# One MoE block on one core: the end of the attention phase in an order of its own, and the first tile loads and pad writes on other engines

## The chip, the core and the metric

One program runs on one core of a Trainium2 chip. The core has a TensorE (matrix products, here PE), VectorE (DVE), ScalarE (ACT), GpSimd (POOL) and SyncE (SP, which here only issues transfers and waits). Each engine takes its own list of instructions in order; they are tied together by semaphores. SP, ACT and POOL issue DMA transfers. The metric is the device time of one execution in microseconds.

## The reference, cut to what matters

Input `x` has 16 images of 256 channels and 14 x 14 pixels. A convolution block runs first, then linear attention over the 196 pixels (tokens) of each image, then a mixture of experts (MoE) over all 3136 tokens. The kernel computes every token for its two chosen experts only.

```python
x = _L0_conv_ref(x, ...)                       # conv 1x1, 3x3, 1x1 with batch norms, residual
t = _to_tokens(x)                              # (16, 196, 256)
t = t + _L1_attn_ref(_ln_t(t), w_qkv, w_out, b_out)   # linear attention, 16 heads of 16
t = t + _L1_ffn_ref(_ln_t(t), gate_w, gate_b, w1, b1, w2, b2)
x = _from_tokens(t, x)

def _L1_ffn_ref(x, gate_w, gate_b, w1, b1, w2, b2):   # E = 8 experts, 1024 hidden columns
    probs = softmax(flat @ gate_w + gate_b)
    top_p, top_i = top_k(probs, 2)
    top_w = top_p / (sum(top_p) + 1e-9)
    for e in range(8):
        h = gelu(flat @ w1[e] + b1[e])
        out = out + comb[:, e:e + 1] * (h @ w2[e] + b2[e])
```

## The kernel before, in words

**Phase A** goes over the 16 images in a software pipeline. Slot `n` of the loop does stage `in` of image `n`, `norm` of `n - 1`, `qkv` of `n - 2`, `soft` of `n - 3`, `ctx` of `n - 4`, `out` of `n - 5`, `norm2` of `n - 6` (the table `LAG`). So in slots 16 to 24 images run out: fewer and fewer stages are left, and the loop keeps its distances. The stages of one image form a chain: `ctx` on PE (L759, 4 matmuls), masked on DVE (`cT`, L1103), `proj` on PE (L768), copied by ACT (`pr`, L578), `out` on PE (L775), added by DVE (`img`, L1110), statistics on DVE (L1027), an inverse root by 13 short dependent DVE steps (L1047 to L1066), normalised by ACT into `rows` (L535), turned on PE (L787), copied by ACT (`xT`, L583), gate logits on PE (L797).

Images go in pairs to the **routing** of a group g = 0 to 7 (392 tokens): `route_choose` on DVE (L1141 to L1148), an exponential on ACT (L587), `route_top` on DVE (L1156 to L1195: the two experts, the count per expert `run`), `route_rank` on PE (L805 to L810), `route_slots` on DVE (L1202 to L1215). A slot is the row of the DRAM table `rows_by_expert` to which a token's row goes. `send_rows` on POOL (L442) then scatters the group by 8 indirect DMAs of 98 rows of 265 floats. Group g is scattered under semaphore number g mod 4.

**The tile table.** When all counts are known, DVE works out in a chain of small instructions (`tile_table`, L1226 to L1296) where each expert's rows end (`pad_at`), at which column of the table each of the 56 tiles of 128 rows lies (`tbi[:,1]`), how many of the first four tiles are full without the last group (`late`, `latei`), each tile's expert (`tbi[:,0]`), and the packed list for PE and DVE (`packedi`, `is_expert`). Behind each expert's last row, 128 rows of `padrow` are written so that the last tile of an expert has defined rows: SP does this with 8 plain DMAs (L353, L354), each behind a register load of its address.

**Phase B** takes the 56 tiles, sorted by expert. For tile m: ACT loads its rows (`load_rows`, L616 to L627, three tiles ahead), PE turns them (`x_turn`, L837), ACT rounds them (`xrTh`, L633), DVE forms the rest (`xrTl`, L1360), PE multiplies by the first matrix (`hidden`, L844, in three parts), DVE adds the bias (L1375), ACT applies gelu (L638), PE turns the result (L871), ACT and DVE split it, PE multiplies by the second matrix (`expert_out`, L844), DVE finishes, POOL adds the rows into the output (L464). PE slot m does `h_turn(m-2)`, `x_turn(m)`, `hidden(m-1)`, `expert_out(m-2)`.

On ACT the loads of tiles 0, 1 and 2 stand ahead of the first `turned` (L633). Each of them reads three values into registers (one from `tbi`, two from `latei`) and waits on semaphores by those values: a tile that is not full without the last group waits for that group's scatter and for all the pads, a full one for neither. By the reference's own routing the first expert gets 936 of the 6272 rows (8 tiles), 718 of them from groups 0 to 5. So tiles 0 to 4 are full without groups 6 and 7, and tile 7 is the expert's last, with 40 rows.

PE starts phase B only when the whole table is done (`s_tab` at `TAB_STEPS`).

## Time and profile before

| | us |
|---|---|
| median of 3 runs without profile | 713.14 (710.79 to 713.86) |
| the profiled execution's own time | 718.35 |
| its span, first to last instruction | 716.6 |
| TensorE, granted clock over the span | 0.923 |

Outside the span lie 1.75 us. The profiled execution took 5.21 us more than the median. Times of the trace count from the start of the span. A row of the time line gives start, duration, engine, line, operation, output<-input, how many such instructions are merged, and in brackets how long the engine was idle before it and who ended that.

### The profile page before, as it was taken

To read this page: it belongs to the slowest core of one execution; us is meant where nothing else is said; L and a number is where in the kernel's file an instruction comes from. 1 tells how busy PE (TensorE), PEld (TensorE's weight loads), DVE (VectorE), ACT (ScalarE), POOL (GpSimd) and SP (SyncE) were. 2 spreads that over 40 slices of the span, in tenths; PEclk is the share of its full clock that TensorE was granted. 3 is DMA by queue.
4 is the path that set the end of the run, shared out by engine and by line. 5 is a ranking of instruction groups with operands and counts; after the bars stand their busy time and mean duration, and the time that the engine had idled before them with its cause. 6 is when DMAs were issued, how large, how long until landed. Compare 5 with 4: busy or idle time off the path is not lost.

```text
span 716.6 us, 13723 instructions
## 1 busy us (share of the span) xinstructions
PE 618.5 (86%) x3884; PEld 544.8 (76%) x3884; DVE 455.6 (64%) x1484; ACT 320.1 (45%) x624; POOL 218.3 (30%) x194
## 2 busy tenths in 40 slices
PE   7664699999999965239999999999999999999982
PEld 3642578888788854228999999999999999999972
DVE  2867879999997864515565565565565565565550
ACT  1475678878775522104343334334334334334330
POOL 6040233224655564621221212221131221221220
PEclk9887699999999985559999999999999999999996
DMA  9418878988979841231246383744726628322211
GB/s 252 155 59 293 335 295 308 316 305 296 329 261 369 336 147 52 87 104 31 46 145 203 49 299 47 248 100 95 253 45 169 187 39 289 67 39 46 31 16 15
DMA packets 50197, 121.09 MB, mean 169 GB/s; under 512 B 7308, under 2 KB 38864, under 8 KB 43984
## 3 DMA queue, kind: packets, MB, share of 16 engines
q1 hardware_dynamic: 30368, 98.54, 38.1%
q0 software_dynamic: 11136, 14.00, 11.5%
q10 hardware_dynamic: 8624, 7.68, 4.1%
q8 instruction: 38, 0.62, 0.3%
q14 instruction: 31, 0.25, 0.1%
HBM read 68.09 MB, written 52.11 MB: 168 GB/s over the span
## 4 chain that ended last, share of the span: by engine, by line
PE 65%; DVE 16%; issue 6%; DMA 4%; ACT 3%; SPq 2%; DVEq 0%; another core or an unknown queue 0%; POOL 0%; ACTq 0%; POOLq 0%
PE ps L844 44%; PE ps L871 6%; DMA wset<-in_ew 3%; DVE wset L1116 3%; PE ps L683 2%; PE ps L738 2%; PE ps L693 2%; PE ps L837 2%; DVE stt L1027 1%; DMA img<-in_x 1%; PE ps L768 1%; PE ps L759 1%; PE ps L775 1%; DVE cT L1103 1%; SPq L353 1%
## 5 line engine op out<-in xcount | busy, mean ns | idle before, releaser
L464 POOL DMA_INDIRECT out<-ys,xr x56 | 86.7, 1548 | 309.2 <-DVE ys L1386 235.8
L844 PE MATMUL ps<-wset,hTh 128*128 x896 | 163.0, 283 | 3.5 <-DVE hTl L1354 3.4
L844 PEld LDWEIGHTS ps<-wset,hTh 128*128 128x128 f32 x896 | 141.6, 190 | 10.2 <-issue 5.5
L844 PE MATMUL ps<-wset,xrTh 128*128 x448 | 146.6, 408 | 0.0
L638 ACT ACTIVATE hb<-hb 128x512 f32<-128x512 f32 x112 | 70.4, 633 | 133.5 <-DVE hb L1375 133.2
L844 PE MATMUL ps<-wset,hTl 128*128 x448 | 126.3, 282 | 0.0
L644 ACT CAST hTh<-ps 128x512 fp32r<-128x512 f32 x112 | 60.3, 590 | 99.1 <-PE ps L871 98.6
L1381 DVE TENSOR_TENSOR yb<-ps,bset 128x256 f32<-128x256 f32 x56 | 23.8, 425 | 125.1 <-PE ps L844 125.1
L844 PEld LDWEIGHTS ps<-wset,xrTh 128*128 128x128 f32 x448 | 80.8, 190 | 15.7
L844 PE MATMUL ps<-wset,xrTl 128*128 x224 | 89.1, 398 | 0.0
L1375 DVE TENSOR_TENSOR hb<-ps,bset 128x512 f32<-128x512 f32 x112 | 75.5, 686 | 16.6 <-PE ps L844 16.3
L844 PEld LDWEIGHTS ps<-wset,hTl 128*128 128x128 f32 x448 | 85.0, 190 | 0.0
L1354 DVE TENSOR_TENSOR hTl<-ps,hTh 128x512 fp32r<-128x512 f32 x112 | 71.8, 683 | 11.5 <-ACT hTh L644 8.7
L442 POOL DMA_INDIRECT rows_by_expert<-rows,slot x64 | 62.4, 975 | 31.1 <-issue 16.6
L418 POOL TENSOR_TENSOR img<-img,bo 98x512 f32<-98x512 f32 x16 | 29.1, 1816 | 109.5 <-ACT xh L535 105.9
L738 PE MATMUL ps<-xT,wq 128*128 128x196 f32 x256 | 51.5, 346 | 12.6 <-ACT vT L557 9.9
L871 PE MATMUL ps<-ident,hb 128*128 128x128 f32 x448 | 58.3, 273 | 0.9 <-ACT hb L638 0.9
L738 PEld LDWEIGHTS ps<-xT,wq 128*128 128x128 f32 x256 | 45.1, 198 | 18.1 <-ACT xT L552 9.6
L871 PEld LDWEIGHTS ps<-ident,hb 128*128 128x128 f32 x448 | 50.2, 141 | 1.6 <-ACT hb L638 1.6
L844 PEld LDWEIGHTS ps<-wset,xrTl 128*128 128x128 f32 x224 | 42.5, 190 | 10.3
L837 PE MATMUL ps<-ident,xr 128*128 128x128 f32 x112 | 22.0, 279 | 20.9 <-DVE packedi L1293 12.5
L775 PE MATMUL ps<-pr,vT 128*98 128x256 f32 x128 | 32.7, 401 | 1.5 <-ACT pr L578 1.5
(196 smaller groups left out, 948.3 us busy)
## 6 DMA issues: line engine op xcount, KB each, us to landing
split_weights<-wset SPq DMA_DIRECT2D x16, 2048.0 KB
wset<-split_weights SPq DMA_DIRECT2D x32, 1024.0 KB
wset<-in_ew SPq DMA_DIRECT2D x16, 1024.0 KB, 10.6
xr<-rows_by_expert ACTq DMA_DIRECT2D x56, 132.5 KB, 2.2
bset<-in_eb SPq DMA_DIRECT2D x8, 640.0 KB
out<-img SPq DMA_DIRECT2D x16, 196.0 KB
img<-in_x SPq DMA_DIRECT2D x6, 392.0 KB, 7.2
rows_by_expert<-padrow SPq DMA_DIRECT2D x9, 132.5 KB
```

Of the source, the lines that this page charges most:

```text
L418: pool.tensor_tensor(t, t, bo2[:, :, :].rearrange("p j d -> p (j d)"), ALU.add).then_inc(S["norm"]["pool"], 1)
L442: pool.indirect_dma_start(norm_rows, bass.IndirectOffsetOnAxis(slot[:, g % 2, k, t:t + 1], 0), rows[:, at, h, :], None).then_inc(s_rows[g ...
L464: pool.indirect_dma_start(out, bass.IndirectOffsetOnAxis(xr[:, r % XR, C + E:ROW].bitcast(U32), 0), ys[:, r % YS, :], None, compute_op=ALU ...
L638: act.activation(hb[:, p, h * 512:(h + 1) * 512], hb[:, p, h * 512:(h + 1) * 512], ACT.Gelu).then_inc(s_ge, 1)
L644: act.copy(hTh[:, p, h * 512:(h + 1) * 512], ps[:, 3 + h, :]).then_inc(s_hhi, 1)
L738: last = pe.matmul(dst[:, h * HW:(h + 1) * HW], wq[:, k, off + h * 128:off + (h + 1) * 128], xT[:, p, k, :], start=(k == 0), stop=(k == 1))
L775: last = pe.matmul(psC[0:HALF, j * C:(j + 1) * C], vT[:, i % 3, h, j * HALF:(j + 1) * HALF], pr[:, i % 2, h, :], start=(h == 0), stop=(h = ...
L837: last = pe.transpose(ps[:, 0, k * 128:(k + 1) * 128], xr[:, b, k * 128:(k + 1) * 128], ident[:, :])
L844: last = pe.matmul(dst, rows_k[:, k * 128:(k + 1) * 128], wset[:, bass.ds(column(k) + rest, width)], start=(k == 0 and n == 0), stop=(k == ...
L871: last = pe.transpose(ps[:, 3 + h, k * 128:(k + 1) * 128], hb[:, p, h * 512 + k * 128:h * 512 + (k + 1) * 128], ident[:, :])
L1354: V.tensor_tensor(hTl[:, p, part], ps[:, 3 + h, :], hTh[:, p, part].bitcast(F32), ALU.subtract).then_inc(s_hlo, 1)
L1375: V.tensor_tensor(hb[:, p, h * 512:(h + 1) * 512], ps[:, 1 + h, :], bset[:, bass.ds(off + h * 512, 512)], ALU.add).then_inc(s_hb, 1)
```

## The change

What it does:

1. **The end of phase A.** The slot loops of PE, ACT and DVE stop at `n = 17` (`TAIL`). What slots 18 to 24 did for images 12 to 15 is written out per engine. `ctx` of image 15 uses its own PSUM bank and stands right behind `proj` of image 14; `proj` of 14, `out` of 15 and `xT` of 15 use other banks too; images 14 and 15 are normalised together. `ones2` and `both` of the routing get two buffers each, and the steps `pos` to `slots` a semaphore of their own.
2. **The flags of the first four tiles** now count rows without the last two groups. Column and flag of two tiles are packed into one integer (`sooni`). ACT loads the two integers, then per tile only waits by the flag and raises `s_soon`; SP issues the loads of tiles 0 to 3, each when its flag is up, and then those of 4 to 7, all of which wait for groups 6 and 7 and for all pads. ACT issues loads from tile 8 on.
3. **The pads** go to POOL: 8 indirect DMAs of 128 rows, in its order behind the last scatter. The pad row block that SP wrote at the start is written by POOL too.
4. **The table.** PE and DVE start phase B when columns and experts are there (`TAB_EXPERTS`, 25 steps). What follows (`schedule_table`) DVE does behind the first tile's `xrTl`; PE waits for `TAB_STEPS` ahead of its fifth slot.

```diff
             sp.wait_ge(s_const, NCONST)
-            sp.dma_start(norm_rows[128 * NONE:128 * (NONE + 1), :], padrow[:, :]).then_inc(s_ends, 16)
...
-            sp.wait_ge(s_ends, 16)
-            sp.wait_ge(s_tab, 1)
-            for e in range(E):
-                at = sp.value_load(pad_at[0:1, e:e + 1], min_val=0, max_val=128 * (NONE - 1))
-                sp.dma_start(norm_rows[bass.ds(at, 128), :], padrow[:, :]).then_inc(s_ends, 16)
-            sp.wait_ge(s_tab, TAB_STEPS)
+            sp.wait_ge(s_tab, TAB_ROWS)
+            soon_two = [sp.value_load(sooni[0:1, n:n + 1], ...) for n in range(SOON // 2)]
+            for i in range(SOON):
+                one = soon_two[i // 2] >> (8 * (i % 2))
+                sp.wait_ge(s_soon, i + 1)
+                load_rows(sp, one & 127, i)
+            for a in range(2, RING // 2):
+                sp.wait_ge(s_rows[a], 256)
+            sp.wait_ge(s_ends, 16 + 16 * E)
+            for i in range(SOON, XR):
+                load_rows(sp, sp.value_load(tbi[0:1, 1, i:i + 1], ...), i)
+            sp.wait_ge(s_tab, TAB_EXPERTS)
...
             send_rows(B // 2 - 1, 1)                                  # gpsimd
+            pool.wait_ge(s_tab, TAB_PADS)
+            for e in range(E):
+                pool.indirect_dma_start(norm_rows, bass.IndirectOffsetOnAxis(pad_at[:, e:e + 1], 0),
+                                        padrow[:, :], None).then_inc(s_ends, 16)
...
-            for i in range(3):                                        # scalar
-                load_rows(i, i)
+            for a in range(2):
+                act.wait_ge(s_rows[a], 256)
+            act.wait_ge(s_tab, TAB_ROWS)
+            soon_two = [act.value_load(sooni[0:1, n:n + 1], ...) for n in range(SOON // 2)]
+            for i in range(SOON):
+                more = (soon_two[i // 2] >> (8 * (i % 2))) & 128
+                for a in range(2, RING // 2):
+                    act.wait_ge(s_rows[a], more + 128)
+                act.wait_ge(s_ends, more + 16)
+                act.sem_inc(s_soon, 1)
...
+            G = B // 2 - 1                                            # tensor
+            out_out(LAST - 2)
+            route_rank(G - 3)
+            norm2_logits(LAST - 4)
+            soft_kT(LAST)
+            ctx_ctx(LAST - 1)
+            ctx_proj(LAST - 1)
+            ctx_ctx(LAST)
+            norm2_xT(LAST - 3)
+            out_out(LAST - 1)
+            ctx_proj(LAST)
+            norm2_logits(LAST - 3)
+            out_out(LAST)
+            route_rank(G - 2)
+            pe.matmul(psV[:, E:2 * E], ones[:, :], run[:, (G - 1) % 2, :], start=True, stop=True)
+            norm2_xT(LAST - 2)
+            norm2_logits(LAST - 2)
+            norm2_xT(LAST - 1)
+            norm2_xT(LAST)
+            norm2_logits(LAST - 1)
+            norm2_logits(LAST)
+            route_rank(G - 1)
+            pe.matmul(psV[:, 0:E], ones[:, :], run[:, (G + 1) % 2, :], ...).then_inc(s_cntp, 1)
+            route_rank(G)
...
-            pe.wait_ge(s_tab, TAB_STEPS)
+            pe.wait_ge(s_tab, TAB_EXPERTS)
...
+            out_add(LAST - 1)                                         # vector
+            wait_for(dve, "out", "vec", "add", LAST - 1)
+            stats("norm2", 1, LAST - 1, n + 2)
+            out_add(LAST)
+            wait_for(dve, "out", "vec", "add", LAST)
+            stats("norm2", 0, LAST, n + 2)
+            beside(inverse_roots(n + 2, 0, 2), route_slots(G - 2))
+            drain(chains[1])
+            drain(route_choose(G - 1))
+            drain(route_top(G - 1))
+            drain(route_choose(G))
+            beside(route_top(G), route_slots(G - 1))
+            drain(chains[1])
+            beside(route_slots(G), tile_table())
+            drain(chains[1])
+            dve.wait_ge(s_tab, TAB_EXPERTS)
...
+                if m == 0:
+                    drain(schedule_table())
```

How it stands on the engines: a name with `<-` is output and input, `x3` is how many like it follow, and the waits are the semaphores of other engines. PE before, from `out` of image 14:

```order
L775 MATMUL ps<-pr,vT 98x256 [waits ctx_steps_of_act]
L775 MATMUL ps<-pr,vT 98x256 x3
L797 MATMUL ps<-gw,xT 98x8 [waits route_steps_of_vec,norm2_steps_of_act]
L797 MATMUL ps<-gw,xT 98x8 x3
L759 MATMUL ps<-qn,ekt 128x128 [waits out_steps_of_vec,soft_steps_of_pool,soft_steps_of_act]
L759 MATMUL ps<-qn,ekt 128x128 x3
L768 MATMUL ps<-wo,cT 128x256 [waits soft_steps_of_act,ctx_steps_of_vec]
L768 MATMUL ps<-wo,cT 128x256
L787 MATMUL ps<-ident,rows 128x98 [waits norm2_steps_of_act]
L787 MATMUL ps<-ident,rows 128x98 x3
L775 MATMUL ps<-pr,vT 98x256 [waits ctx_steps_of_act]
L775 MATMUL ps<-pr,vT 98x256 x3
```

PE now, from `proj` of image 14:

```order
L813 MATMUL ps<-wo,cT 128x256 [waits in_steps_of_act,ctx_steps_of_vec]
L813 MATMUL ps<-wo,cT 128x256
L799 MATMUL ps<-qn,ekt 128x128 [waits soft_steps_of_vec,soft_steps_of_pool,soft_steps_of_act]
L799 MATMUL ps<-qn,ekt 128x128 x3
L841 MATMUL ps<-ident,rows 128x98 [waits route_steps_of_vec,gate_steps_of_act,norm2_steps_of_act]
L841 MATMUL ps<-ident,rows 128x98 x3
L824 MATMUL ps<-pr,vT 98x256 [waits ctx_steps_of_act]
L824 MATMUL ps<-pr,vT 98x256 x3
L813 MATMUL ps<-wo,cT 128x256 [waits soft_steps_of_act,ctx_steps_of_vec]
L813 MATMUL ps<-wo,cT 128x256
L851 MATMUL ps<-gw,xT 98x8 [waits route_steps_of_vec,gate_steps_of_act]
L851 MATMUL ps<-gw,xT 98x8 x3
```

`ctx` of image 15 (the row with `qn,ekt`) has moved ahead of `out` of image 14 and has lost its wait for DVE's add of image 14.

ACT before, behind its last instruction of phase A (`latei` holds the flags):

```order
L616 TENSOR_LOAD tbi [waits rows_sent_to_experts2,rows_sent_to_experts1,padding_written,rows_sent_to_experts0,table_steps]
L616 ISA x2
L618 TENSOR_LOAD latei
L618 ISA x2
L618 TENSOR_LOAD latei
L618 ISA x2
L627 ISA [waits expert_ends_padded,rows_sent_to_experts3]
L627 DMA xr<-rows_by_expert 128x265
```

ACT now at the same place (one tile's flag; three more follow, then `xrTh` of tile 0):

```order
L688 TENSOR_LOAD sooni [waits table_steps,rows_sent_to_experts1,rows_sent_to_experts0]
L688 ISA x2
L688 TENSOR_LOAD sooni
L688 ISA x2
L692 REGISTER_ALU x2
L693 REGISTER_ALU [waits rows_sent_to_experts3,rows_sent_to_experts2]
L692 REGISTER_ALU [waits expert_ends_padded]
```

The three address and flag loads per tile and the DMA issue are gone from ACT; two loads for all four tiles are left.

POOL now, from the last group's scatter:

```order
L464 DMA rows_by_expert<-rows,slot 26752x265 [waits place_steps_of_vec,token_numbers_written]
L464 DMA rows_by_expert<-rows,slot 26752x265 x7
L478 DMA rows_by_expert<-padrow,pad_at 26752x265 [waits table_steps]
L478 DMA rows_by_expert<-padrow,pad_at 26752x265 x7
L489 DMA out<-ys,xr 3264x256 [waits residual_written,padding_written,expert_rows_ready]
```

Between the scatter and the first add of expert rows now stand the eight pad writes.

## Rows read from the trace of the kernel before

**Rows 1.** The page: the span, and the granted clock in 40 slices of it:

```profile
span 716.6 us, 13723 instructions
...
PEclk9887699999999985559999999999999999999996
```

**Rows 2.** The chain that ended last (start, us): turning of tiles 1, 4, 5:

```profile
317.18 0.66 PE ps L837 x2
...
338.63 0.22 PE ps L837 x2
...
345.39 0.22 PE ps L837 x2
```

**Rows 3.** The time line, tiles 0 to 2: loads, turning, first rounding:

```profile
304.51 11.58 ACTq L627 DMA_DIRECT2D xr<-rows_by_expert  x3
...
308.16 0.69 PE L837 MATMUL ps<-ident,xr 128*128 128x128 f32 x2 [12.54 <-DVE packedi L1293]
...
316.13 0.37 ACT L633 CAST xrTh<-ps 128x256 fp32r<-128x256 f32 x1 [24.36 <-DMA rows_by_expert<-padrow]
```

**Rows 4.** The instructions on xr from 294 to 345: landing of tile loads:

```profile
DMA to landing us min/median/max: 2.0/2.6/3.9
```

**Rows 5.** Instructions by line, min/median/max ns: register work and pad writes from 294 on:

```profile
L618 ACTq TENSOR_LOAD <-latei x2: 278/280/282, 303.2 to 303.7; - x2
...
L618 ACTq TENSOR_LOAD <-latei x1: 1396/1396/1396, 308.1 to 308.1; - x1
...
L354 SPq DMA_DIRECT2D rows_by_expert<-padrow x8: 3/332/700, 298.1 to 316.3; - x8
```

**Rows 6.** The time line, PE, DVE and ACT at the end of phase A:

```profile
254.36 0.61 DVE L1103 SCALAR_TENSOR_TENSOR cT<-ps,kx,heads 128x128 f32<-128x128 f32 x2 [0.84 <-PE ps L759]
...
255.02 1.87 PE L768 MATMUL ps<-wo,cT 128*128 128x256 f32 x4 [1.55 <-DVE cT L1103]
...
260.94 1.13 PE L759 MATMUL ps<-qn,ekt 98*128 98x128 f32 x8 [0.26 <-DVE img L1110]
...
264.97 0.61 DVE L1103 SCALAR_TENSOR_TENSOR cT<-ps,kx,heads 128x128 f32<-128x128 f32 x2 [1.56 <-remote]
...
269.83 3.73 PE L775 MATMUL ps<-pr,vT 128*98 128x256 f32 x8 [1.47 <-ACT pr L578]
...
280.09 0.35 DVE L1047 TENSOR_SCALAR sm<-mv 98x2 f32<-98x2 f32 x1
...
280.09 1.50 PE L797 MATMUL ps<-gw,xT 128*98 128x8 f32 x8 [0.57 <-ACT xT L583]
...
283.38 0.16 DVE L1066 SCALAR_TENSOR_TENSOR sm<-mv,sm 98x2 f32<-98x2 f32 x1 [0.17 <-DVE sm L1063]
284.15 1.09 ACT L535 ACTIVATE rows<-img,sm 98x256 f32<-98x256 f32 x2 [4.11 <-DVE sm L1066]
...
292.67 0.17 DVE L1191 TENSOR_TENSOR run<-run,rv 98x8 f32<-98x8 f32 x1
...
295.65 0.19 DVE L1202 TENSOR_TENSOR rt<-ps,expert_row 98x32 f32<-98x32 f32 x1 [2.69 <-issue]
```

**Rows 7.** The time line, DVE in the tile table:

```profile
300.32 0.16 DVE L1267 TENSOR_SCALAR latei<-late 128x4 int32<-128x4 f32 x1
300.51 0.69 DVE L1271 TENSOR_REDUCE tb<-big 128x64 f32<-128x512 f32 x1
```

**Rows 8.** The time line, POOL: scatters, first of groups 5 and 7, last:

```profile
276.97 0.97 POOL L442 DMA_INDIRECT rows_by_expert<-rows,slot  x1 [9.29 <-DVE slot L1215]
...
300.67 0.98 POOL L442 DMA_INDIRECT rows_by_expert<-rows,slot  x1 [0.30 <-POOL rows L435]
...
309.53 0.96 POOL L442 DMA_INDIRECT rows_by_expert<-rows,slot  x1 [0.30 <-issue]
```

**Rows 9.** The page: all scatters (L442) and adds (L464), mean ns in the middle:

```profile
L464 POOL DMA_INDIRECT out<-ys,xr x56 | 86.7, 1548 | 309.2 <-DVE ys L1386 235.8
...
L442 POOL DMA_INDIRECT rows_by_expert<-rows,slot x64 | 62.4, 975 | 31.1 <-issue 16.6
```

More of the change, by code:

```diff
@@ L546, in norm2_norm @@
                     act.wait_ge(s_rows[g % (RING // 2)], 128 * (g // (RING // 2) + 1))
-                normalise("norm2", 1, i, n, [rows[:, i % RING, j, 0:C] for j in range(2)])
+                normalise("norm2", which, i, n, [rows[:, i % RING, j, 0:C] for j in range(2)])
             def norm_xT(i):
@@ L780, in norm2_xT @@
                 wait_for(pe, "norm2", "act", "norm1", i)
-                wait_for(pe, "norm2", "act", "xT", i - 1)
+                bank = psL
+                if i < LAST:
+                    wait_for(pe, "gate", "act", "xT", i - 1)
+                else:
+                    bank = psT
+                    wait_for(pe, "ctx", "act", "proj", LAST - 1)
                 if i % 2 == 0:
@@ L1121, in over, with step @@
                 return v.unsqueeze(2).to_broadcast([HALF, 4, k])
[L1123 to L1127 removed]
+            L, comb, pos = rt[:, 0], rt[:, 5], rt[:, 6]
+            def step(name, g, reads=None, stage="route"):
                 if reads is not None:
[L1129 to L1134 removed]
+                    wait_for(dve, stage, "vec", reads, g)
+                done_r[stage] += 1
+                assert after(stage, "vec", name, g) == done_r[stage]
+                return S[stage]["vec"], 1
+            done_r = {"route": 0, "place": 0}
             def route_choose(g):
                 v = rv[:, g % 2]
[L1139 removed]
+                wait_for(dve, "gate", "pe", "logits", 2 * g + 1)
                 sig = step("bias", g)
@@ L1204, in route_slots @@
                 yield
-                sig = step("prods", g, "pos")
+                sig = step("prods", g, "pos", "place")
                 V.tensor_tensor(rt[:, 7:9], pos.unsqueeze(1).to_broadcast([HALF, 2, 4, E]), ones2,
@@ L1299, in tile_table @@
                 dve.wait_ge(s_tab, tab[0])
-            for n in range(SLOTS_A):
+            for n in range(TAIL):
                 i = {stage: n - LAG[stage] for stage in LAG}
```

223 lines of the change are left out of this document (140 added, 83 removed).

## The prediction

> **What bounds the kernel now.** I read the page first. The span is 716.6 us, and the granted clock stands at five tenths from slice 15 to 17, that is from about 268 to 322 us: full clock 2.4 GHz, there 1.2 [rows 1]. That stretch is the end of phase A and the start of phase B, the place of the change. Behind it everything runs in a fixed beat: the chain that ended last turns tile 4 at 338.63 and tile 5 at 345.39, one tile in 6.76 us [rows 2], to the end. No instruction of that beat is changed. So the whole question is when the beat starts, and the marker is the turning of tile 1, at 317.18 [rows 2].
>
> What holds tile 1 back? Tile 0 was turned at 308.16 already, yet ACT rounded it only at 316.13 [rows 3], because ACT was still issuing loads: three of them spread from 304.51 to 316.09 [rows 3]. One register load of ACT takes 278 ns at 303 us and 1396 ns at 308 [rows 5]; SP's eight pad writes stretch from 298.1 to 316.3 [rows 5]; the two-matmul turn of tile 0 shows 0.69 us where those of tiles 4 and 5 show 0.22 [rows 2, 3]. I call this the **crawl**: from about 300 to 313 us several engines advance in steps of 0.7 us. It goes on just as long as POOL scatters group 7, from 300.67 to 310.49 [rows 8], and a little longer. Ahead of it, the table of tiles waits for the counts: `run` of group 7 is written at 292.67, its `pos` at 295.65 [rows 6], the flags at 300.32 [rows 7]. ACT gets free of its waits at about 302, when group 6 has landed.
>
> **The change part by part.** The sum is made in times of the profiled execution (718.35, 1.75 outside the span); that one is 5.21 above the median of 713.14.
>
> *Order of the tail.* `proj` of image 14 ends at 255.02 + 1.87 = 256.9 [rows 6]. `ctx` of image 15 stood at 260.94, behind the add of image 14 [rows 6]; now it follows `proj` directly. Its 1.13 us may double to 2.1 at the lower clock, and DVE sees it 0.84 later, so `cT` of image 15 comes at 260.0 and not 264.97 [rows 6]: 5.0 earlier. From there: `proj` 15 (1.9, copy 0.9, waits 1) and `out` 15 (3.73 [rows 6]) put the add at about 269, both statistics at 270.7. The 13 root steps take 283.54 - 280.09 = 3.4 [rows 6]: 274.1. Two images are normalised one behind the other, 2 x 1.09 [rows 6]: 276.4. Turning, copying and the logits of 14 and 15 (1.50 each [rows 6], halves overlapping): 280.3. The rank product of group 6 stands ahead on PE, 1.9: 282.2. Top-two work of group 7 to `run`: 285.7, against 292.84, so 7 us gained; `pos`, 2.8 behind it as before (2.98 - 0.17 [rows 6]): 288.5.
>
> *The table.* From `pos` to the flags 300.48 - 295.65 = 4.8 before [rows 6, 7]. One reduction of 0.69 [rows 7] now stands ahead of the flags, and a packing step of about 0.2: 5.75, hence 294.2.
>
> *First load.* ACT waits only for groups 4 and 5 for tiles 0 to 3 (the reference's counts fill those tiles without the last two groups), reads two integers of 0.28 each [rows 5] with their register work (1.4 in all, estimated from three reads and an issue per tile at the uncrawled rate), checks the flag (0.5); SP issues (0.3) and the rows land 2.6 later, the middle of 2.0 to 3.9 [rows 4]: tile 0 is turned at 299.0. ACT has no loads left in front of its rounding. Before, rounding to the next turn took 317.18 - 316.13 = 1.05 [rows 2, 3], the turn itself and its lag 0.5 more: **tile 1 is turned at 300.4 and not 317.18, 16.8 earlier.** Of this 7 is the tail, less 1 for the longer table; the other 10.7 is ACT's wait for group 6 and the crawl over its nine reads and three issues.
>
> *What is moved behind tile 0 on DVE* (`schedule_table`, some 15 small instructions, 2.6) lies under the first hidden product, whose operands DVE has given up by then; PE asks for it only ahead of its fifth slot. Nothing. If the cover fails it costs at most 2.6.
>
> *POOL.* The scatter of group 5 waited 9.29 for its slots at 276.97 [rows 8]; with slots at 271.6 it starts at 272.1. A group takes 309.53 + 0.96 - 300.67 = 9.82, 0.3 between instructions [rows 8], plus the copies: group 5 to 282.2, group 6 283.9 to 294.0, group 7 294.5 to 304.6. Then eight pads of 128 rows. None is in this trace. By the mean scatter of 98 rows, 975 ns [rows 9], unscaled: 0.98 + 0.3 = 1.28 each, the floor. By the mean add of 128 rows, 1548 ns [rows 9]: 1.85, the ceiling. I take the scatter scaled by rows, 975 x 128/98 + 300 = 1.57, as the same kind of write: 8 x 1.57 = 12.6, to 317.2 (314.8 to 319.4). They land 2.0 later as a load's minimum does [rows 4], SP reads and issues 0.6, tile 4 lands 2.6 later: 322.4. Its turn falls due at 338.63 - 16.8 = 321.8. So the gate of tile 4 costs 0.6 (below zero at the floor, 2.8 at the ceiling, up to 4.7 if landing also takes its longest). POOL's adds start behind the pads at 317.2; the first result comes two tiles after 300.4, near 316, so they are late by a microsecond or two, and ring buffers absorb that.
>
> Here a rule speaks against the change. SP issued the first two pads, before the crawl, about 2 us apart, and one write shows 332 ns of issue in the middle [rows 5]; POOL's nearest kind shows 975 [rows 9]. The Trainium skill (DMA: Bandwidth & Descriptors, "Issuing engine by pattern") puts plain stores on Sync and says of the two ways that the one from SP and ACT is "generally faster". By that rule the pads left on SP would finish with group 7's landing, tile 4 would have 11 us to spare, and the 0.6 of the gate would be 0; the sum hardly moves, the risk does.
>
> Sum in the profiled execution: -16.8 + 0.6 = **-16.2**, 702.1.
>
> *From the profiled execution to the median.* The profiled one is 5.21 slower, by more than the 3.07 that the three runs span. Outside the crawl nothing in the trace looks stretched, so I take those 5.2 us to be the crawl, absent or weaker in the timed runs. The changed kernel has its first four loads issued by 297 and would not pay it; the timed gain is then 16.2 - 5.2 = 11.0, and the median **702.1**. In words of the skill: the Trainium skill (NOTIFIC — the notification-queue block, "7.1 Overflow: three behaviours, one of which stalls the engine") says that the record path's inner pipeline always backpressures and can throttle an engine; that would make the crawl the profiler's own. No row here proves it.
>
> **The rivals.** *(a) The crawl is real* and is in the timed runs too; the 5.2 is some other overhead of a profiled run. Then the median falls by the full 16.2, or 15 to 19 with the landing bounds: 694 to 698, say 697. For it: the crawl coincides with scatters, and earlier groups' scatters may do the same unseen. Against: the earlier scatters from 276.97 to 300.1 run beside ACT and DVE rows of ordinary length (0.16, 0.17, 1.09 [rows 6]).
>
> *(b) The crawl is real and lies on POOL's write stream behind the table, wherever that is.* It begins about when the table is read and ends with POOL's last scatter. POOL's stream now ends not at 310.5 but with the eighth pad, at 317.2, and the crawl ends 2.5 to 3.7 behind it (before, it held ACT until 316.1 with scatters ending at 310.5). If it holds ACT's two reads, four flag checks and the rounding in the same way, tile 1 is turned at 319 to 321 and not 317.2: 3.7 us **slower**, 716.8. It decides from the point where the crawl reaches back before 297. Against: ACT has 2 reads to make, not 9, and SP only 2; even at 1.4 us each they cost 2 more.
>
> *(c) POOL is the bound:* pads at or above the ceiling of 1.85, or groups 5 to 7 late because the tail gains less than 5 on DVE's side. Then tile 4 comes at 327 to 330 and the beat starts late by 5 to 8: 706 to 710. For it: my margin is below zero already. It holds too where SP's waits, in program order, hold the loads of tiles 4 to 7 all together, so that the last of them comes 2 us later still.
>
> *(d) The tail doesn't move:* DVE, which now does both adds, both statistics and the top-two work of group 5 in one written order, or PE at half clock, is late, and `run` stays at 292.8. Then tile 1 still comes at 307.5, POOL stays as it was and its pads end at 323: tile 4 at 328.5, late by 0 against 338.63 - 10 = 328.6; gain 10 in the profile, 5 in the median: 708.
>
> **How the numbers follow.** The forecast of 702.1 (its own range 699 to 706: the landing 2.0 to 3.9, the pads 1.28 to 1.85, the tail +-2) gets 0.46. (a) 0.22, (c) 0.14, (d) 0.09, (b) 0.09. The range reaches from 695 (inside (a)) to 710 (inside (c)); outside it are (b) and the edges of (a) and (c), together 0.2. A measurement of this kernel can tell about 0.5%, 3.6 us, from no change, so faster means below 709.6: the forecast, (a), (d) and nearly all of (c), 0.84 with a rest for what I have not seen; within 0.5%: part of (c), of (d) and half of (b), 0.09; slower 0.07.
>
> **What would show it.** In the profile of the changed kernel: `cT` of image 15 near 260 (order of the tail); `run` of group 7 near 285.7; SP's first load near 296.5; tile 1 turned near 300.4; ACT's register loads at 0.28, or at 1.4 if the crawl has come along; eight pad writes on POOL from 304.6 to 317.2, their mean the number that I bounded; a wait of PE or ACT at tile 4 of a microsecond or none; the first adds near 317. If tile 1 is turned early and tile 4 late, it is (c); if tile 1 is at 307, (d); if it is at 319, (b). The excess of the profiled execution over the median says whether the crawl was the profile's: near 0 for my reading, near 5 for (a). I am wrong altogether if the beat of 6.76 itself changes, or if the low clock lasts longer into phase B.

## The result and the profile after

The changed kernel took 715.36 us (713.32 to 717.67, 20 runs), the kernel before 711.69 in 20 runs beside it. The ratio, formed over the rounds, is 1.0042, interval 1.0028 to 1.0056: 3.0 us slower (the two medians lie 3.7 apart). The forecast was 702.1 and faster; the time lies outside the range of 695 to 710. What came is the size of rival (b): slower by 3.7.

The page of the kernel after, its span and the granted clock:

```profile
span 714.7 us, 13676 instructions
...
PEclk9987799999989986568999999999999999999997
```

The clock is granted at or near its lower level (1.2 GHz, five and six tenths) in about the same place as in [rows 1]. The time line of the kernel after, all engines, from 299 to 325 us (`issue` and `remote` in the brackets mean that the view names no engine or transfer of this core that ended the wait):

```profile
299.79 26.09 SPq L268 DMA_DIRECT2D xr<-rows_by_expert  x8
...
302.18 0.66 PE L917 MATMUL ps<-ident,xr 128*128 128x128 f32 x2 [11.05 <-DMA xr<-rows_by_expert]
...
306.20 0.37 ACT L660 CAST xrTh<-ps 128x256 fp32r<-128x256 f32 x1 [18.62 <-DMA rows_by_expert<-rows,slot]
...
307.25 0.66 PE L917 MATMUL ps<-ident,xr 128*128 128x128 f32 x2 [4.41 <-DVE xrTl L1493]
...
308.84 1.49 POOL L478 DMA_INDIRECT rows_by_expert<-padrow,pad_at  x1 [0.30 <-issue]
...
311.31 0.40 PE L924 MATMUL ps<-wset,xrTl 128*128 x1
...
311.47 0.68 DVE L1508 TENSOR_TENSOR hb<-ps,bset 128x512 f32<-128x512 f32 x1
...
318.29 0.96 POOL L478 DMA_INDIRECT rows_by_expert<-padrow,pad_at  x1 [0.30 <-issue]
321.69 0.69 DVE L1508 TENSOR_TENSOR hb<-ps,bset 128x512 f32<-128x512 f32 x1 [9.54 <-remote]
...
324.01 0.63 PE L917 MATMUL ps<-ident,xr 128*128 128x128 f32 x2
```

Read it from the top. Tile 0 is turned at 302.18, 6.0 earlier than in [rows 3], tile 1 at 307.25, 9.9 earlier than in [rows 2]. Then all is lost again. PE's last product of tile 0's hidden layer ends at 311.7. DVE adds the bias to the first half at 311.47 and is free at 312.15. The second half waits by the program for that product alone, and DVE takes it up only at 321.69, 9.5 us late. ACT and PE still work off the first half, until 313.5; from then on to 321.5 nothing runs but POOL and SP's last steps. POOL's eighth pad is issued at 318.29 and ends at 319.25; 2.4 us later the work goes on. Tile 2 is turned at 324.01, 16.8 behind tile 1; before, it followed by 6.7, at 323.8. The chain of the kernel after shows where the beat begins:

```profile
324.22 0.43 PE ps L917 x2
...
340.15 0.22 PE ps L917 x2
```

The last row is tile 4: 340.15 against 338.63 [rows 2], 1.5 later. From there the beat is 6.72 a tile, as it was before from tile 5 on.

The same thing on a smaller scale stands at the end of phase A. The time line of the kernel after, DVE and PE around the logits of the last two images:

```profile
277.71 2.72 PE L851 MATMUL ps<-gw,xT 128*98 128x8 f32 x16
...
285.17 0.19 DVE L1224 TENSOR_TENSOR rt<-ps,gb 98x32 f32<-98x32 f32 x1 [5.34 <-remote]
...
288.59 0.18 DVE L1275 TENSOR_TENSOR run<-run,rv 98x8 f32<-98x8 f32 x1
```

The logits end at 280.4, and DVE takes them up at 285.17, 4.7 later. POOL's scatters of group 5 run from 273.98 to 283.7. I call this, and the crawl of the prediction, the **hold**.

The lines of SP's loads in the kernel after, one form each (min/median/max ns, first and last start):

```profile
L268 SPq DMA_DIRECT2D xr<-rows_by_expert x7: 6/333/700, 299.8 to 324.5; - x7
L268 SPq ALU_OP  x6: 3/358/1397, 299.0 to 310.3; - x6
```

The steps of 0.7 and 1.4 us of [rows 5] are there again, now on SP. They go on to 315. Yet the hold is not there at every moment of POOL's run. POOL writes without a break from 298.80 to 319.25, and between 306.2 and 313.5 ACT, DVE and PE hand work to each other at their usual pace; DVE's eight small steps of the schedule (307.02 to 308.7) come 0.2 apart. In the kernel before, DVE's steps at that place stood 0.7 apart. What starts and ends a single held stretch is not shown.

### The profile page after: what moved, and what is told of

The parts are those of the page before. It is cut to its first block, busy times and chain, and to the rows that moved or that the text cites. A ratio compares the mean times of both kernels' runs of the same rounds, so it can differ in the third digit from the quotient of the medians.

```text
span 714.7 us, 13676 instructions
## 1 busy us (share of the span) xinstructions
PE 616.1 (86%) x3884; PEld 544.1 (76%) x3884; DVE 456.0 (64%) x1471; ACT 320.1 (45%) x624; POOL 228.7 (32%) x205
## 4 chain that ended last, share of the span: by engine, by line
PE 67%; DVE 19%; issue 5%; ACT 2%; another core or an unknown queue 2%; DMA 2%; DVEq 1%; POOL 0%; SPq 0%; ACTq 0%; POOLq 0%
PE ps L924 43%; PE ps L951 7%; DVE wset L1199 3%; PE ps L773 2%; PE ps L718 2%; PE ps L728 2%; PE ps L708 2%; DVE stt L1108 2%; PE ps L917 2%; PE ps L799 2%; DMA wset<-in_ew 1%; PE ps L824 1%; PE ps L762 1%; DVE cT L1185 1%
## 5 line engine op out<-in xcount | busy, mean ns | idle before, releaser
L464 POOL DMA_INDIRECT rows_by_expert<-rows,slot x64 | 61.5, 961 | 30.3 <-issue 16.9
L951 PE MATMUL ps<-ident,hb 128*128 128x128 f32 x448 | 58.7, 274 | 10.7 <-ACT hb L665 10.7
L440 POOL TENSOR_TENSOR img<-img,bo 98x512 f32<-98x512 f32 x16 | 30.7, 1919 | 110.5 <-ACT xh L560 110.5
L773 PE MATMUL ps<-xT,wq 128*128 128x196 f32 x256 | 51.6, 347 | 12.2 <-ACT vT L582 10.9
L773 PEld LDWEIGHTS ps<-xT,wq 128*128 128x128 f32 x256 | 45.1, 199 | 17.7 <-ACT xT L577 9.4
L924 PEld LDWEIGHTS ps<-wset,xrTl 128*128 128x128 f32 x224 | 42.8, 191 | 10.4
L762 PE MATMUL ps<-wq,xT 128*98 128x256 f32 x128 | 33.9, 412 | 0.0
```

Source lines behind the costliest of these rows:

```text
L440: pool.tensor_tensor(t, t, bo2[:, :, :].rearrange("p j d -> p (j d)"), ALU.add).then_inc(S["norm"]["pool"], 1)
L464: pool.indirect_dma_start(norm_rows, bass.IndirectOffsetOnAxis(slot[:, g % 2, k, t:t + 1], 0), rows[:, at, h, :], None).then_inc(s_rows[g ...
L762: last = pe.matmul(psQ[0:HALF, j * C:(j + 1) * C], xT[:, p, k, j * HALF:(j + 1) * HALF], wq[:, k, 0:C], start=(k == 0), stop=(k == 1))
L773: last = pe.matmul(dst[:, h * HW:(h + 1) * HW], wq[:, k, off + h * 128:off + (h + 1) * 128], xT[:, p, k, :], start=(k == 0), stop=(k == 1))
L924: last = pe.matmul(dst, rows_k[:, k * 128:(k + 1) * 128], wset[:, bass.ds(column(k) + rest, width)], start=(k == 0 and n == 0), stop=(k == ...
L951: last = pe.transpose(ps[:, 3 + h, k * 128:(k + 1) * 128], hb[:, p, h * 512 + k * 128:h * 512 + (k + 1) * 128], ident[:, :])
```

## The experiments

All ratios are against the kernel before, timed on the same chip in the same rounds. The other columns, in us, are from one profiled execution each: the start of group 5's first write, and the turning of tiles. That execution and the timed median can differ by a few microseconds; the ratio decides.

The column of group 5 shows why. Six of these kernels have the same program up to that write, but for buffers set aside and a constant written at the start: before, before with 8 more, with 8 more of 16 rows, with 8 more paced, with pauses by four, and with POOL busy otherwise. Still it comes anywhere from 270.4 to 277.0, and the profiled execution of the kernel before is the latest. The profiled executions of the six lie above or below their own medians nearly in that order: 270.4 (-3.4 us), 271.9 (-1.6), 272.2 (-2.4), 272.9 (-0.9), 275.3 (+3.0), 277.0 (+5.2, or +6.7 by all 20 runs). So when two kernels are compared by their tiles, what they already differ by in this column comes off first. (The gaps of work put 1.8 us of POOL's own work ahead of it.)

| kernel | ratio (95% interval) | group 5 | tile 1 | tile 2 | tile 4 |
|---|---|---|---|---|---|
| before | 1 | 277.0 | 317.2 | 323.8 | 338.5 |
| after | 1.0042 (1.0028 to 1.0056) | 274.0 | 307.2 | 324.0 | 340.0 |
| after, pads on SP | 0.9887 (0.9858 to 0.9916) | 273.5 | 307.9 | 315.7 | 330.3 |
| after, 8 more writes | 1.0159 (1.0129 to 1.0189) | 273.3 | 309.0 | 326.0 | 349.3 |
| before, new tail alone | 0.9988 (0.9969 to 1.0007) | 271.1 | 312.3 | 320.0 | 334.7 |
| before, 8 more writes | 1.0104 (1.0074 to 1.0134) | 271.9 | 321.5 | 328.3 | 343.1 |
| before, 8 more of 16 rows | 1.0117 (1.0080 to 1.0155) | 272.9 | 322.4 | 330.3 | 345.0 |
| before, 8 more, paced | 1.0021 (0.9995 to 1.0048) | 272.2 | 315.0 | 322.8 | 337.5 |
| pads on SP, group 7 later | 0.9854 (0.9819 to 0.9888) | 274.2 | 304.3 | 312.0 | 326.8 |
| pads on SP, old tail | 0.9957 (0.9930 to 0.9984) | 272.6 | 310.0 | 317.2 | 331.8 |
| **pads on SP, pauses by four** | **0.9788 (0.9755 to 0.9821)** | 271.2 | 296.3 | 303.4 | 318.0 |
| before, pauses by four | 0.9967 (0.9944 to 0.9991) | 270.4 | 306.8 | 314.4 | 329.0 |
| after, pauses by four | 0.9975 (0.9953 to 0.9997) | 271.9 | 297.0 | 303.9 | 331.8 |
| before, POOL busy otherwise | 0.9996 (0.9972 to 1.0020) | 275.3 | 314.8 | 321.6 | 336.2 |
| pads on SP, pauses by eight | 0.9859 (0.9822 to 0.9896) | 273.7 | 303.7 | 311.2 | 326.1 |
| pads on SP, gaps of work | 0.9816 (0.9786 to 0.9846) | 275.1 | 299.6 | 306.5 | 324.8 |

### Where the time went: pads, stream or tail

**The pads back on SP.** The edit is which engine writes them (the block written at the start too):

```diff
                 load_rows(sp, one & 127, i)
+            for e in range(E):
+                at = sp.value_load(pad_at[0:1, e:e + 1], ...)
+                sp.dma_start(norm_rows[bass.ds(at, 128), :], padrow[:, :]).then_inc(s_ends, 16)
...
-            for e in range(E):                                        # gpsimd
-                pool.indirect_dma_start(norm_rows, ... pad_at[:, e:e + 1] ..., padrow[:, :], None).then_inc(s_ends, 16)
```

> The changed kernel, but the eight pads are plain DMAs of SP again, issued behind its loads of tiles 0 to 3 (the first pad block at the start is SP's too). Theory A (the crawl): SP, DVE and ACT are held as long as POOL's stream of indirect writes runs; it now ends with group 7 near 308.5, so the crawl ends near 311 and not at 321.5, tile 2 is turned near 314 to 316 and not at 324.0, tile 4 near 332: 7 to 8 us faster than the changed kernel, about 708, 3 to 4 faster than before. Theory B (only the gate of tiles 4 to 7 decides, the crawl is the profile's own): the pads on SP land near 317 to 318 and not 321, tile 4 comes 3 earlier at most: about 712 to 713. Theory C (the tail's new order alone makes the kernel slow): still 715.

Measured 0.9887: by the ratios 8.1 us faster than before and 11 faster than the changed kernel. This is theory A's number and more; the gate alone (theory B) would have given 3. The chain of this kernel:

```profile
307.87 0.66 PE ps L916 x2
...
315.83 0.22 PE ps L916 x2
...
330.42 0.22 PE ps L916 x2
```

Tile 1 is turned at nearly the same time as in the changed kernel (0.6 later), tile 2 8.3 earlier. POOL's stream ends at 308.4 here. The eight pads stand on SP from 311.4 to 320.2, behind the hold, at 1.1 us each.

**Eight more writes**, which nobody reads or waits for, in the kernel after and in the kernel before:

```diff
+            for e in range(E):
+                pool.indirect_dma_start(spare[e], ... padrow[0:128, C + E:ROW] ..., padrow[0:128, :], None).then_inc(s_extra, 16)
```

> The changed kernel with eight further indirect writes of 128 rows on POOL, into tables that nobody reads, behind the pads; only POOL itself waits for them, at its own end. Theory A: the crawl lasts 10.2 us longer, to about 331.7; tile 2 is turned near 334; about 10 us slower than the changed kernel, 725. Theory B: nobody waits for them, and POOL's first add is not due before 333: 715, no change.

> The kernel before with eight further indirect writes of 128 rows on POOL behind the last scatter, into tables that nobody reads; only POOL waits for them, at its own end. Theory A: the crawl ends at about 323 and not 313, tile 1 is turned near 327 and not 317; about 10 us slower than before, 721.5. Theory B: nobody waits for them and POOL's first add is due only near 330: 711.7, no change.

Measured 1.0159 and 1.0104. Against the changed kernel the first is 1.17% or 8.3 us slower, the second 7.4 us slower than before. Theory B said no change. The expected 10 us were a little too many, and the expected place was wrong: in the kernel after, tile 2 came through at 326.0 and not at 334, and the further hold fell on tile 3 (341.4). Its time line:

```profile
323.67 0.69 DVE L1514 TENSOR_TENSOR hb<-ps,bset 128x512 f32<-128x512 f32 x1 [9.70 <-remote]
...
333.50 1.07 ACT L677 CAST hTh<-ps 128x512 fp32r<-128x512 f32 x2 [8.47 <-remote]
```

POOL writes without a break here until 328.7. DVE was let go in the middle of that run, work went on to 330.9, and ACT took up PE's next result only 4.8 us behind the run's end. So a longer run makes more hold, but one held stretch need not end with the run. In the time line of the kernel before with eight more, ACT issues its three loads here:

```profile
300.01 20.41 ACTq L633 DMA_DIRECT2D xr<-rows_by_expert  x3
```

20.4 us for three loads, where [rows 3] has 11.6. Nothing was changed on ACT. POOL's last of the eight starts at 314.40. Tile 1 is turned 4.3 later than before, though group 5 had begun 5.1 earlier.

**The tail alone**: the kernel before with the new order of PE, ACT and DVE and, but for what the flags count, nothing else of the change (the diff is the part of the change above from `G = B // 2 - 1` to `tile_table()`).

> The kernel before with the new order of the end of phase A alone: loads of tiles by ACT, pads by SP and the whole table ahead of phase B as before (the flags count without the last two groups, which changes none for tiles 0 to 3). Theory A: the counts of group 7 come 4 us earlier (288.8 against 292.8), group 7's scatters end near 308.5 and not 310.5, the crawl near 311 and not 313: tile 1 turned near 315, 2 us faster than before, about 709.7. Theory B: tile 1 is earlier by the 4 us of the counts: 707.7. Theory C: slower than before by 3.

Measured 0.9988, an interval that holds 1. In the profiled execution tile 1 came 4.8 earlier and tile 4 3.7, but group 5 had begun 5.9 earlier already; the timed runs show 0.9 us, not told from zero. Theory C (the tail makes it slow) is out. **The pads on SP with the old tail** is the other half of that question (the diff is e1's without the order of the tail; ACT there waits for the flags, as in the change):

> The version with the pads on SP, but with the old order of the end of phase A: loads by SP, flags without the last two groups, the rest of the table behind tile 0. The counts come 3 to 4 us later again, and so do group 7's scatters (end 310.5). If the gain of the pads-on-SP version is that ACT has no addresses and loads to work through in the hold, it keeps most of it: 0.992 of before (5 to 6 us faster). If the tail's order is what brings it, it is 0.997 or worse.

Measured 0.9957, between the two expectations. So loads by SP with the short flags are worth 3 us without the new tail (interval 1 to 5), and the tail 5 us more (0.9957 to 0.9887) once the loads no longer stand in its way. Together they give 8 us, more than the 4 of each alone; by the intervals the difference is between 1 and 7.

### What in POOL's stream does it

**Short writes, paced writes, no writes**, all in the kernel before, all behind the last scatter:

```diff
-    ... padrow[0:128, C + E:ROW] ..., padrow[0:128, :], None)         # eight more
+    ... padrow[0:16, C + E:ROW] ..., padrow[0:16, :], None)           # of 16 rows
```

```diff
+                if e:                                                 # paced
+                    pool.wait_ge(s_extra, 16 * e)
```

```diff
+            for e in range(16):                                       # busy otherwise
+                pool.tensor_scalar(idle[:, 1, :], idle[:, 0, :], 2.0, None, ALU.mult).then_inc(s_extra, 1)
+                pool.wait_ge(s_extra, e + 2)
```

> As the run with eight further writes of 128 rows in the kernel before (which took 1.04% more than it), but each of the eight writes only 16 rows, an eighth of the bytes and descriptors. If the hold comes from POOL being at work on indirect writes at all, and one of 16 rows takes POOL about as long as one of 98 or 128 (0.96 and 0.97), it still costs 7 to 8 us: 719. If it comes from the bytes or the number of rows, about 1 us: 712.5. If a short write is issued in half the time, 3 to 4 us and the hold still ends with the stream.

> The kernel before with eight further writes of 128 rows as before, but each waits until the one ahead has landed (some 3.3 us apart, to about 335). If any write of POOL under way holds the others, the hold lasts until about 337 and the time grows by more than with the unpaced ones, over 10 us. If only a stream without gaps holds them, no more than 0 to 3 us are lost.

> The kernel before with POOL busy for about 10 us behind the last scatter, with sixteen small products of its own on 128x512 elements and no writes. If it is indirect writes that hold the others, no change: 1.000 of before. If any work of POOL does, about 7 us slower, 1.010.

Measured 1.0117, 1.0021 and 0.9996. A write of 16 rows takes POOL 0.85 and not 0.97, and costs the others the same, so it is neither the bytes nor the rows. The same eight writes at a distance of 3 us cost nothing that can be told from zero. And POOL at its own work costs nothing, though its sixteen products, each waiting for the one ahead, took 25.1 us and not 10:

```profile
308.96 25.14 POOL L458 TENSOR_SCALAR idle<-idle 128x512 f32<-128x512 f32 x16
```

SP's steps show the same in the profiles. Its own pad writes from 312 us on, in the kernels with eight more writes, with paced ones and with POOL busy otherwise, in this order:

```profile
L356 SPq MOVE rows_by_expert<-padrow x4: 3/29/688, 312.0 to 321.1; - x4
...
L356 SPq MOVE rows_by_expert<-padrow x2: 29/29/29, 312.2 to 313.3; - x2
...
L356 SPq MOVE rows_by_expert<-padrow x3: 29/29/29, 312.1 to 314.2; - x3
```

Only in the first do steps of 0.7 us go on behind 312 (the last on any engine starts at 318.4); in the other two the last starts at 310.3, 4.8 and 1.4 us behind the end of the last scatter, though POOL's paced writes go on to 329 and its products to 334.

What holds the others is an **unbroken run of indirect writes on POOL**.

### Breaking the stream

**Group 7 later** sends the last group only once tile 1 is turned; **pauses by four** wait for the landing of the four writes ahead:

```diff
+                if g == B // 2 - 1 and j == 0:                        # group 7 later
+                    pool.wait_ge(s_eT, 2)
```

```diff
+                if g >= B // 2 - 3:                                   # pauses by four
+                    if j:
+                        pool.wait_ge(s_rows[g % R], 128 * (g // R) + 64)
+                    else:
+                        pool.wait_ge(s_rows[(g - 1) % R], 128 * ((g - 1) // R + 1))
```

> The version with the pads on SP (0.989 of before), but POOL sends group 7 only once tile 1 is turned. Theory A1 (writes hold engines that wait, and hardly those that work): nothing is held between 298 and the turning of tile 1, which comes near 303 and not 307.9; group 7 goes out beside the running beat, to 313, tile 4 loads near 318, due 325: 5 us faster than the version with the pads on SP, about 0.982 of before. Theory A2 (writes hold everybody at any time): tile 1 comes near 303, but tile 2 is held until about 315: about the same as the pads on SP, 0.989.

> The version with the pads on SP, and POOL's stream broken in groups 5 to 7: ahead of each four writes it waits until those before have landed, 2 to 3 us each time. If only an unbroken stream holds the others, the hold near 282 (3.6 us, PE to DVE) and that near 300 to 307 both go: the counts come 3 us earlier, tile 1 is turned near 300; group 7 ends near 317 and tile 4 loads near 323, where it may wait 2 us. 6 us faster than the pads on SP alone: 0.980 of before. If the pauses only delay the groups, tile 4 is late by 8 and it is no faster than before.

Measured 0.9854 and 0.9788. The second is 15 us faster than the kernel before and 18 faster than the changed one. In group 7 later, tile 1 comes at 304.3, and the eight writes run beside the beat from 305.84 to 316.14 with little harm (tile 2 at 312.0, and tile 3 at 319.7, 7.7 behind it, where the version with pauses has 6.8; theory A1). With the pauses both holds are gone. The time line of the version with pauses:

```profile
277.70 0.19 DVE L1229 TENSOR_TENSOR rt<-ps,gb 98x32 f32<-98x32 f32 x1 [0.70 <-PE ps L856]
...
281.80 0.17 DVE L1280 TENSOR_TENSOR run<-run,rv 98x8 f32<-98x8 f32 x1
...
292.20 2.34 SPq L268 DMA_DIRECT2D xr<-rows_by_expert  x4
294.59 0.66 PE L922 MATMUL ps<-ident,xr 128*128 128x128 f32 x2 [10.26 <-DMA xr<-rows_by_expert]
...
296.33 0.66 PE L922 MATMUL ps<-ident,xr 128*128 128x128 f32 x2 [1.08 <-issue]
```

DVE takes up the logits 0.7 after it is free, and not 5.3. `run` of group 7 is written at 281.80: 10.9 earlier than in [rows 6], 6.8 earlier than in the changed kernel; of these, 5.8 and 2.8 were there at group 5's first write, ahead of the first pause that cost anything. SP issues four loads in 2.34 us. Tile 1 follows tile 0 by 1.7. This is the kernel without the hold that the prediction's sum describes, except that here the pads are on SP.

The same pauses in the two given kernels:

> The kernel before with these pauses alone. If only an unbroken stream holds the others: ACT works through its loads at 1.1 us each from about 305 (group 6 lands later by 3), tile 1 is turned near 309 to 311 and not 317; tile 4 waits for group 7, which lands near 320: 4 to 6 us faster than before, 0.993. If not: slower by the pauses' 3 to 6 us.

> The changed kernel with the pauses in groups 5 to 7 and in the pads too. The hold goes, tile 1 comes near 300 and tile 2 near 308 and not 324; but the pads now end near 333, tiles 4 to 7 load near 337, so tile 4 is turned near 339 by the gate alone, as in the changed kernel (340.0): within 2 us of it. That would say that pads on POOL cannot win either way.

Measured 0.9967 and 0.9975. The hold is gone from both profiles (tile 1 at 306.8 and 297.0). In the kernel before the timed gain is 2.3 us, less than expected, though the profiled execution had tile 4 9.4 earlier. The column of group 5 settles that difference: 6.6 us of it were there ahead of the first pause that cost anything, and 2.8 remain. In the changed kernel, where the pauses also stand ahead of the first and the fifth pad, the pads on POOL become the gate, plainly. Its chain:

```profile
325.87 2.60 DMA rows_by_expert<-padrow,pad_at
...
329.28 2.52 DMA xr<-rows_by_expert
...
331.85 0.69 PE ps L925 x2
...
341.59 0.22 PE ps L925 x2
```

Tile 3 was turned at 310.7. Tile 4 waits 21 us for the last pad, its landing and its own load, and PE, idle for 13 us, is back near the lower clock (0.69 granted on average from 331 to 342, 1.00 from 342 to 350), so that tile 5 takes 9.7. So with the hold the pads on POOL cost 11 us of the timed ratio, by the hold, and without it 13, by the gate.

**How long a run it takes, and what ends it:**

```diff
-                if g >= B // 2 - 3:
-                    if j: ... else: ...
+                if g >= B // 2 - 3 and j == 0:                        # pauses by eight
+                    pool.wait_ge(s_rows[(g - 1) % R], 128 * ((g - 1) // R + 1))
```

```diff
+                if g >= B // 2 - 3:                                   # gaps of work, ahead of each four
+                    pool.tensor_scalar(idle[:, 1, :], idle[:, 0, :], 2.0, None, ALU.mult).then_inc(s_extra, 1)
+                    breaks[0] += 1
+                    pool.wait_ge(s_extra, breaks[0])
```

> The version with the pads on SP and a wait for the landing only ahead of each group of eight writes (in the run with pauses ahead of each four: 0.979 of before, tile 1 turned at 296.3). If the hold needs more than eight writes in a row, it is as good or better, since group 7 ends 2 to 3 us earlier: 0.977 to 0.980. If it sets in within eight, the hold near 280 (group 5's writes) is back and the counts come 3 us later, and tile 1 later still: 0.984 to 0.988.

> The version with the pads on SP and 1.6 us of other work on POOL ahead of each four writes, without a wait for their landing (2 to 3 us with the waits). If a gap in the issue is enough to end the hold, as good as the run with pauses: 0.979, or 1 us better. If the writes under way must run dry, which takes some 2 us, the hold stays in part: 0.983 to 0.989.

Measured 0.9859 and 0.9816. With eight in a row the hold of group 5 is back: nothing starts but on POOL from 281.9 to 285.0, when seven of group 5's writes (from 273.67) are out; DVE could have gone on at 280.1, behind the sixth. `run` of group 7 comes at 288.44 again. Group 7's eight in a row (300.65 to 310.5), beside the running beat, delay the hand-overs of PE, ACT and DVE by a microsecond at most, or little more; only SP takes steps of 0.7 us. With a gap of 1.5 us filled with POOL's own work, ahead of each four, that hold is gone: `run` at 285.00 in that profile, and no silence. So a break in the issue is enough for most of it, landed or not. Not for all: in the last four writes (308.84 to 313.6) of this version, DVE takes up a product that PE ended at 312.5 only behind the last of them:

```profile
314.83 0.42 DVE L1522 TENSOR_TENSOR yb<-ps,bset 128x256 f32<-128x256 f32 x1 [4.35 <-remote]
```

PE then runs dry for 2.8 us, falls back towards the lower clock (0.70 granted from 319.3 to 325), and tile 4 comes 11.5 behind tile 3 and not 7.8. The intervals of the two versions overlap; which kind of break is better is not settled.

## Why the prediction was wrong, point by point

The sum for tile 4 was -16.8 for the marker and +0.6 for the gate. In the profile of the kernel after tile 4 is turned at 340.15 and not at 322.4, 17.7 late: 6.9 of it had come about by tile 1, and 10.8 between tiles 1 and 4. Two steps failed. The sum credited the change with all of the crawl over ACT's reads and issues (10.7 of the 16.8), and it charged eight more writes in POOL's stream with nothing but the gate (0.6). The timed runs price the second at 11 us: with the pads off POOL the ratio is 0.9887.

- **The base of the sum was one late execution.** The prediction measures the tail's gain from `run` at 292.84 and finds 7 us. In the other profiles with the old tail and no pauses `run` of group 7 is written at 287.5, 287.8, 288.5, 288.6 and 290.9; in the six with the new tail and groups 5 and 6 unbroken at 285.8 to 289.0. So of the 7 us at most one or two are the order's, and the timed runs agree (0.9 us, not told from zero). Here is `cT` of image 15 in the kernel before with pauses, whose program up to this point is that of the kernel before:

```profile
260.49 0.61 DVE L1109 SCALAR_TENSOR_TENSOR cT<-ps,kx,heads 128x128 f32<-128x128 f32 x2
```

  It stands at 264.97 in [rows 6] and was forecast to move to 260.0.
- **Order of the tail: met until the logits, in part by luck.** `cT` of image 15 came at 260.59 (forecast 260.0), the roots ended at 274.8 (274.1), both images were normalised at 276.9 (276.4), the logits done at 280.4 (280.3). The times are right, the gain over the kernel before is mostly that of the late base. The next step failed: "Top-two work of group 7 to `run`: 285.7". It came at 288.6, because DVE stood 5.34 us in the hold of group 5's scatters. With pauses it is 281.8.
- **The table: right.** From `pos` at 291.17 to the flags at 296.69: 5.5, forecast 5.75.
- **First load: failed in size.** "ACT waits only..., reads two integers" at unheld rates gave tile 0 at 299.0 and tile 1 at 300.4. In the held state it was 302.2 and 307.2: the flag checks of ACT went on to 306.2. The prediction knew of the crawl, tied it to POOL's scatters, and still priced the first loads without it, since they were to be issued by 297. They were issued from 299.8, behind the start of group 7's writes.
- **What lies behind tile 1: missing.** The sum took tile 1 as the marker and the beat as fixed behind it. The marker was met in part (9.9 of 16.8 us) and the beat then broke between tiles 1 and 2, where DVE stood for 9.5 us. "POOL's adds start behind the pads ... ring buffers absorb that" looked for the harm of eight further instructions in POOL's own queue; it was in everybody else's.
- **The pads' price: the floor.** I took 1.57 each. They took 1.28 apart, 0.97 for 128 rows, nearly as much as for 98 (the first 1.49): 10.4 in all, from 308.84 to 319.25. The gate of tile 4, on which much of the text went, was covered by the hold.
- **A row misread.** The prediction counts the turn of tile 0 (0.69 us, against 0.22 for tiles 4 and 5) among the signs of the crawl. The 0.22 is the chain's part of that turn; the time line has 0.38. And tile 1's turn at 317.18, behind the crawl, still takes 0.66. The clock granted there is five tenths: the longer turn is the clock's.
- **From the profiled execution to the median: right in size, wrong in its reason.** I took the 5.21 us by which the profiled execution of before was over the median to be the crawl, absent from the timed runs, and not to be gained there. The size came out: the profiled execution of after is 1.9 us faster than that of before, the timed runs are 3.0 slower, 4.9 between them, and the excess of the profiled execution of after is 1.1, the sign that was named for this reading. But the hold is in the timed runs: adding to POOL's stream moved them by 7 to 8 us, and breaking it took 7 off (0.9887 to 0.9788). And "outside the crawl nothing in the trace looks stretched" was wrong. Most of the excess lies ahead of group 5's first write, between group 4's first write and group 5's: 19.4 us, against 14.3 in the kernel before with pauses, which has none in group 4. The hold has a part in it. Group 4's scatters end at 267.48, and ACT copies `pr` at 269.19, 1.5 us behind the end of its product; in the kernel with pauses it did so at once (second row):

```profile
269.19 0.59 ACT L578 COPY pr<-ps 128x512 f32<-128x512 f32 x1 [4.60 <-PE ps L768]
...
263.27 0.59 ACT L584 COPY pr<-ps 128x512 f32<-128x512 f32 x1 [1.52 <-PE ps L774]
```

- **The rule on plain stores** that the prediction weighed, from the Trainium skill (DMA: Bandwidth & Descriptors, "Issuing engine by pattern"), was priced at 0.6 us. The trace agrees with its direction; its worth here was 11 us, and the reason is not the faster issue of SP (1.1 us each, against 1.28), but that POOL's run of writes gets shorter.
- **The rivals.** (b) named the mechanism (the crawl ends with POOL's last write, and the pads are eight more), the direction and nearly the size, 3.7 for 3.0; it erred in the place, since tile 1 got through and tile 2 was held. I gave it 0.09, on the ground that ACT and SP had few reads left. That was an argument on one victim; the stream had others. (a) was right that earlier groups' scatters hold as well, and rested on the hold being escaped. (c) did not come. (d) has its sign, tile 1 at 307, but not its mechanism: `run` came at 288.6 and not at 292.8. That sign did not tell (d) from a hold.

What stays open: why a run of indirect writes on POOL stops the other engines' steps and waits; whether the signal of the engine ahead comes late or the held engine takes its next instruction late, since no run separates the two; what starts and ends one held stretch within a run; and whether the same would be seen in an execution of which no record at all is made. No run here tells.

## What to carry to other kernels

When a trace shows several engines stepping in equal, too long units, find the engine that alone keeps its pace, and suspect the length of its run of being a cost for all; moving more work onto it is then the wrong direction, however idle it looks. A suspicion of this kind is cheap to test in the timed runs before a change is built on it: append useless work of that kind, and see whether the time moves. A marker (here tile 1) carries a sum only if nothing behind it depends on the resource that is being changed. And a sum that starts from one profiled execution inherits its luck: compare its milestones with those of a second execution of the same program.

## What the runs showed of the hardware

- Indirect writes that GpSimd issues back to back, 1.26 us apart, hold the other engines: a step of SP that takes 0.3 us or less takes 0.7 or 1.4, and in the kernel after DVE took up finished products 4.7 and 9.5 us late. With eight in a row in group 5 it set in behind the sixth or seventh. Runs of four between waits for the landing brought no such wait of PE, ACT or DVE in three profiles; runs of four between gaps of 1.5 us did once, for 2.4 us.
- The held stretches do not cover the whole run, and their ends vary: 1.5 us behind the last write (283.7, 285.2), 2.4 (319.25, 321.7), 4.8 (328.7, 333.5), and once in the middle of a run (323.7).
- Engines that had work in hand mostly ran on at their usual pace, and in two versions eight such writes ran beside the full beat with little harm.
- Rows and bytes hardly matter: 0.85 us for 16 rows, 0.96 for 98, 0.97 for 128, and the same cost to others. Other work of GpSimd, 25 us of it, held nobody.
- Waiting for the landing ahead of each four writes removes it, 1.5 us of other work most of it. With the pads on SyncE that made a kernel 2.1% faster than the one before (1.8 to 2.4).
- Executions differ without any edit: group 5's first write came at 270.4 to 277.0 in six profiles of kernels that are the same up to it. A hold beside group 4's writes is a part of that.
